# Mixing the modes of eight images in two parts on one Trainium2 core

## The reference

```
# layer 0: a dynamic 3x3 filter per image and group of channels
pooled = x.mean(axis=(2, 3))
lf = tanh(batchnorm(pooled @ conv_w.T))               # 9 taps for each of 8 groups
low = sum over taps of lf * shifted x (reflect padding)
x = (low * (inside + 1) - inside * mean(x)) * lamb_l + x * (lamb_h + 1)
# layer 1: a spectral mix of channels, then a blur
X = dht_2d(x)[:, :, :20, :20]                         # Hartley transform, 20 x 20 modes kept
Y = compl_mul2d(X, w1)                                # for each mode, a 32 x 32 mix of channels
y = dht_2d(Y padded to 128 x 128) / (128 * 128)
y = gaussian blur of y, radius 4, over all four axes  # images, channels, rows, columns
return y * (abs(fftfreq(128)) <= 0.25)                # columns outside the band are zero
```

## Time and profile before

| what | value |
|---|---|
| time, median of 3 runs | 151.3 us (150.71 to 153.71) |
| the profiled execution | 152.74 us |
| its span, first to last instruction | 150.9 us |
| PE busy | 125.7 us (83%), 2308 matmul entries |
| DVE, ACT, POOL busy | 79.8, 40.3, 55.3 us |
| moved by DMA | 37.04 MB |
| mean granted TensorE clock | 0.965 of full speed |

### The profile page before, as it was taken

The page is one execution under the profiler, slowest core; times in us unless marked ns, Lnnn a source line. Parts: engine busy times, 40 slices in busy tenths (PEclk is TensorE's granted clock), DMA queues, the critical chain, the costliest instruction groups (busy, mean ns, idle before and its releaser), DMA issues.

```text
span 150.9 us, 5209 instructions
## 1 busy us (share of the span) xinstructions
PE 125.7 (83%) x2308; PEld 71.9 (48%) x2308; DVE 79.8 (53%) x162; ACT 40.3 (27%) x92; POOL 55.3 (37%) x75
## 2 busy tenths in 40 slices
PE   6496558999999999999899797798797987999500
PEld 5132412655463626257567796465463654654200
DVE  0014840856497969595678114664846748444400
ACT  3000410011112020202599311343242423432300
POOL 8980000399876969699974000000000000000000
PEclk9999997589999999999999999999999999999995
DMA  3999999999999998000000000066998989999994
GB/s 99 358 359 321 295 347 362 348 349 372 371 363 380 351 351 273 11 2 4 0 2 0 4 4 4 4 213 242 312 365 300 384 300 329 350 376 380 386 386 158
DMA packets 34839, 37.04 MB, mean 245 GB/s; under 512 B 1162, under 2 KB 34260, under 8 KB 34816
## 3 DMA queue, kind: packets, MB, share of 16 engines
q1 hardware_dynamic: 34816, 36.70, 72.5%
HBM read 19.92 MB, written 16.78 MB: 243 GB/s over the span
## 4 chain that ended last, share of the span: by engine, by line
PE 28%; POOL 27%; DVE 13%; SPq 9%; DMA 9%; issue 8%; ACT 1%; POOLq 0%; DVEq 0%
PE ps L524 11%; POOL acc L870 5%; DMA x_ring<-x 5%; POOL rows L892 5%; SPq L315 5%; PE ps L464 4%; POOL spread L868 4%; PE ps L485 4%; DVE mixed L789 4%; PE ps L505 4%; DMA out<-rows 4%; DVE xht L726 4%; POOL row_prod L840 3%; POOL eo L878 2%; DVE rows L552 2%
## 5 line engine op out<-in xcount | busy, mean ns | idle before, releaser
L370 PE MATMUL ps<-x_ring,k_lt 64*64 64x512 f32 x256 | 34.7, 646 | 6.9 <-DMA x_ring<-x 6.9
L524 PE MATMUL ps<-cols,k_inv 128*64 128x330 f32 (+1 forms) x192 | 31.5, 466 | 4.5 <-DVE rows L552 4.0
L688 DVE STREAM_TRANSPOSE y_sb<-ps 128x1024 f32<-128x1024 f32 x16 | 19.5, 1241 | 18.2 <-PE ps L370 18.2
L524 PEld LDWEIGHTS ps<-cols,k_inv 128*64 128x64 f32 x192 | 13.3, 136 | 18.3 <-issue 11.8
L552 DVE COPY rows<-ps 128x330 f32<-128x330 f32 (+1 forms) x24 | 12.1, 522 | 12.1 <-PE ps L524 10.6
L388 PEld LDWEIGHTS ps<-y_sb,k_t 64*64 64x64 f32 x512 | 15.5, 143 | 5.0 <-DVE y_sb L688 2.7
L388 PE MATMUL ps<-y_sb,k_t 64*64 64x128 f32 x512 | 17.2, 288 | 0.4 <-ACT kb L589 0.4
L552 ACT COPY rows<-ps 128x330 f32<-128x330 f32 (+1 forms) x24 | 11.0, 462 | 23.7 <-PE ps L524 21.9
L370 PEld LDWEIGHTS ps<-x_ring,k_lt 64*64 64x64 f32 x256 | 8.7, 141 | 16.5 <-issue 9.1
L359 PE MATMUL ps<-idle 128*128 128x256 f32 x52 | 14.6, 431 | 1.2 <-DVE idle L657 1.2
L359 PEld LDWEIGHTS ps<-idle 128*128 128x128 f32 x52 | 10.5, 211 | 3.2 <-DVE idle L657 1.2
(11 more groups left out here) (70 smaller groups left out, 133.4 us busy)
## 6 DMA issues: line engine op xcount, KB each, us to landing
x_ring<-x SPq DMA_DIRECT2D x32, 512.0 KB, 8.7
out<-rows SPq DMA_DIRECT2D x16, 640.0 KB, 5.0
out<-rows SPq DMA_DIRECT2D x8, 768.0 KB, 6.2
w_sb<-mix_w SPq DMA_DIRECT2D x2, 960.0 KB, 10.1
k_inv<-inv SPq DMA_DIRECT2D x1, 386.0 KB, 8.6
k_t<-t SPq DMA_DIRECT2D x1, 256.0 KB, 7.2
k_basis<-basis SPq DMA_DIRECT2D x1, 240.0 KB
k_coef<-coef SPq DMA_DIRECT2D x4, 25.4 KB
```

The costliest lines, as they stand in the source:

```text
L370: last = mm(ps[64 * m:64 * m + 64, 2 * hs + g, :], k_lt[64 * g:64 * g + 64, 64 * r:64 * r + 64], x_ring[64 * g:64 * g + 64, u, k:k + 4, r, ...
L524: last = mm(ps[64 * g:64 * g + 64, B_F[k % 3], 0:nt * NW], inv(O_LH + s * H + r * H // 2, (1, H // 2)), cols[:, u, 6 * g:6 * g + nt, :], s ...
L688: nc.vector.transpose(view(y_sb[:, n % 2, 0, 8 * hs, 0:1], (KINDS, 8), (KINDS * HC, 4), (1, 32)), view(ps[:, 2 * hs, 0:1], (1, 1024))).the ...
```

## The change

The mixing is split. `mixin` keeps 9 columns (8 blurred sums and raw image 5, FIRST = 9), and `mixin_late` takes raw images 6 and 7 (LATE = 2), with `mixed` and `mixed_late` behind them. The first mixing runs in four parts amid the chain that makes the taps and modes of image 7. The late mixing runs in four parts between the first outputs' transforms, as 120 further matmuls of 16 columns. Two of the three `eo` planes move from POOL to DVE. Of the 26 keep_busy matmuls, 14 go. ACT alone copies the parts of both mixings. PSUM banks are dealt anew, the gap memset of DVE moves ahead of the products of image 7, and `shares` takes the raw images from two tiles. The order of the output stage is written out for images 0 and 1, and is the loop above from image 2 on.

```diff
-NCOLS = N + N - BLURRED
+FIRST = N + 1
+LATE = N - BLURRED - 1
@@ the tensor engine's program
             coefficients(N - 2)
             logits(N - 1)
-            keep_busy(4)
-            select(N - 1)
-            keep_busy(2)
-            coefficients(N - 1)
-            keep_busy(8)
-
+            keep_busy(6)
             pe.wait_ge(inv_here, 16)
-            pe.wait_ge(terms_done, N)
-            keep_busy(4)
...
-            pe.wait_ge(placed_act, 4)
-            pe.wait_ge(placed_dve, 3)
+            pe.wait_ge(placed_act, 1)
+            pe.wait_ge(placed_dve, 1)
+            mix(0)
+            select(N - 1)
+            mix(1)
+            coefficients(N - 1)
+            mix(2)
+            mix(3)
...
-            pe.wait_ge(mixed_dve, 2)
-            pe.wait_ge(mixed_act, 2)
+            pe.wait_ge(mixed_act, 4)
             turn(0)
-            keep_busy(2)
+            mix_late(0)
             await_modes(0)
             to_columns(0, 0)
             turn(1)
-            for n in range(N):
+            pe.wait_ge(terms_done, N)
+            pe.wait_ge(row_coef_done, N)
+            to_rows(0, 0, 0, next_columns=True)
+            mix_late(1)
+            to_columns(1, 1)
+            to_rows(0, 0, 1)
+            mix_late(2)
+            mix_late(3)
+            to_rows(1, 1, 0)
+            turn(2)
+            to_rows(1, 1, 1)
+            await_modes(2)
+            to_columns(2, 0)
+            turn(3)
+            for n in range(2, N):
@@ the new late mixing, on the tensor engine
+            def mix_late(part):
+                if part == 0:
+                    pe.wait_ge(late_act, 2)
+                    pe.wait_ge(late_dve, 1)
+                hi, bh = part // 2, part % 2
+                for b in range(5 * bh, 5 * bh + 5):
+                    for q in range(Q):
+                        at = (hi * B10 + b) * 8 * LATE
+                        grp = (hi * Q + q) * B10 + b
+                        for s in range(S):
+                            last = mm(ps[q * C:(q + 1) * C, B_LATE, at:at + 8 * LATE],
+                                      w_sb[:, s * GRP + grp, :], mixin_late[:, grp, 1 - s:3 - s, :, :],
+                                      start=(s == 0), stop=(s == 1))
+                last.then_inc(late_mix_done, 1)
@@ the vector engine's program
+            dve.wait_ge(acc_done, BLURRED)
+            tt(view(eo[:, 0, 1, 0:1], (1, N), (3 * N, GRP)), plus, minus, ALU.add).then_inc(eo_done, 1)
+            tt(view(eo[:, 0, 2, 0:1], (1, N), (3 * N, GRP)), minus, plus, ALU.subtract).then_inc(eo_done, 1)
             total(N - 3)
             turn_columns(N - 1)
+            dve.wait_ge(eo_done, 3)
+            dve.wait_ge(zeroed, 2)
+            place_blurred(nc.vector.tensor_copy, 2)
+            place_blurred(nc.vector.tensor_copy, 3)
+            place(0).then_inc(placed_dve, 1)
             products(N - 2)
             total(N - 2)
@@ the scalar engine's program
+            place(0).then_inc(placed_act, 1)
+            spread_taps(N - 1)
             keep_kb(N - 1)
+            for part in range(4):
+                if part == 2:
+                    keep_row_coef(N - 1)
+                    place(1).then_inc(late_act, 1)
+                act.wait_ge(mix_done, part + 1)
+                unmix(nc.scalar.copy, part // 2, part % 2).then_inc(mixed_act, 1)
+            place(2).then_inc(late_act, 1)
```

More of the change, by code:

```diff
@@ L568, in place_blurred @@
             part = slice(C * cl, C * cl + C)
-            return copy(view(mixin[part, 0, 0, beside(cl), 0:1], (4 * NCOLS, 3 * GRP), (1, N)),
+            return copy(view(mixin[part, 0, 0, beside(cl), 0:1], (4 * FIRST, 3 * GRP), (1, N)),
                         view(eo[part, 0, 0, 0:1], (N, 3 * GRP), (1, N)))
@@ L573, in place_raw @@
             part = slice(C * cl, C * cl + C)
-            return copy(view(mixin[part, 0, 0, beside(cl), N + i:N + i + 1], (4 * NCOLS, 3 * GRP)),
-                        view(eo_raw[part, i, 0, 0:1], (1, 3 * GRP)))
+            if i == 0:
+                to = view(mixin[part, 0, 0, beside(cl), N:N + 1], (4 * FIRST, 3 * GRP))
+            else:
+                to = view(mixin_late[part, 0, 0, beside(cl), i - 1:i], (4 * LATE, 3 * GRP))
+            return copy(to, view(eo_raw[part, i, 0, 0:1], (1, 3 * GRP)))
         @block.scalar
@@ L602, in _ @@
             act.wait_ge(spreads_done, 2)
-            for n in range(1, N + 1):
+            for n in range(1, N):
                 if n >= 2:
@@ L645, in _ @@
             modes_step(1, 1)
-            for n in range(N):
+            rows_step(0, (0, 2))
+            cols_step(1, 1)
+            rows_step(0, (4,))
+            unmix_late_step(0)
+            unmix_late_step(1)
+            rows_step(1, (0, 2))
+            modes_step(2, 0)
+            rows_step(1, (4,))
+            cols_step(2, 0)
+            modes_step(3, 1)
+            for n in range(2, N):
                 rows_step(n, (0, 2))
@@ L739, in place @@
                     last = place_raw(nc.vector.tensor_copy, i, cl)
-                last.then_inc(placed_dve, 1)
+                return last
             turn_rows(0, 0)
@@ L814, in _ @@
             modes_step(1, 1)
-            shares(2)
-            for n in range(N):
+            shares(2, raws[:1])
+            rows_step(0, (1,))
+            cols_step(1, 1)
+            rows_step(0, (3, 5))
+            shares(2, raws[1:])
+            rows_step(1, (1,))
+            modes_step(2, 0)
+            shares(3, raws)
+            rows_step(1, (3, 5))
+            cols_step(2, 0)
+            modes_step(3, 1)
+            shares(4, raws)
+            for n in range(2, N):
                 rows_step(n, (1,))
@@ L870, in blur, with first_plane @@
                 tt(acc[:, lo:hi, :], acc[:, lo:hi, :], spread[:, lo:hi, :], ALU.add).then_inc(acc_done, 1)
[L872 removed]
+            def first_plane():
                 pool.wait_ge(acc_done, BLURRED)
[L874 to L878 removed]
+                tt(view(eo[:, 0, 0, 0:1], (1, N), (3 * N, GRP)), view(acc[:, 0, 0:1], (PLANE, N), (1, GRP)),
+                   view(acc[:, 0, GRP:GRP + 1], (PLANE, N), (1, GRP)), ALU.subtract).then_inc(eo_done, 1)
             def raw_planes(n):
```

133 lines of the change are left out of this document (70 added, 63 removed).

## The result

The changed kernel took **155.38 us**, the median of 4 runs (155.16 to 157.22), against 152.24 us for the kernel before in the same set (4 runs, 150.71 to 153.71). The ratio is 1.0317, 95% interval 1.0179 to 1.0454: slower, clear of noise, though the interval leaves open whether by more than 2%. Single executions of a kernel fall into a faster and a slower group some 2 us apart; a ratio compares the faster ones of both kernels in one set, a median takes all. The prediction had 149.3 us and a range of 145.2 to 152.8. It was wrong, on the wrong side, and outside its range.

What follows compares the result with a forecast made beforehand. Loading of PE's 256-instruction blocks was taken to bound the early outputs: from 77.65 us, 15.0 + 17.6 us reach turn(4) at 110.25 against 112.2. Saving 2 us from the 151.3 us median gave 149.3 us, range 145.2 to 152.8.

Steps and rivals of the forecast that it cites:

- main idea: PE runs in blocks of 256 instructions; waiting for their loading sets the time from the first mixing to turn(4).
- rival without blocks: First rival: blocks don't bind from the mixing to the output loop, so 5.8 us come out, 145.5 us; chance 0.27.
- First mixing 76.6, turn(0) 84.3 us: End of input stage: mixing starts at 76.6 us against 83.97, and turn(0) at 84.3 us, 7.3 us early.
- Hold of POOL by DVE, 1.3 us: Borders of image 5: POOL is held while DVE makes two planes, adding 1.3 us (bounds 0 and 2.5).
- The four quiet blocks, 15.0 us, as the chain: From the boundary at 77.65 us in the first mixing: four blocks of 3.75 us, to 92.65 us.
- The four loaded blocks, 4.4 us each: From 92.65 us to turn(4), beside outputs: four blocks of 4.4 us (between 3.75 and 4.65), 17.6 us, to 110.25.
- The ceiling of 5.1 us: Blocks beside outputs: the most one takes if its packet waits longer, where 4.65 us was the usual loaded price.
- From turn(4) on the loop has its old pace: Output loop behind 110.25 us: unchanged pace, so the 2 us gained by turn(4) come out at the end.
- The clock as a rival of its own: Third rival: TensorE half clock from 84 to 93 us costs 2 to 3 us, 152 us; chance 0.07.
- The second rival: Blocks beside outputs cost 5.1 us each, 152.2 us, or 153.4 with dearer planes; chance 0.14.
- 89.1 + 13.6 us: Without code loading: to_rows(0) at 89.1 us plus 13.6 us of PE work puts to_rows(2) at 102.9 us.

Runs made afterwards that it cites:

- 24: Changed kernel with 6 small one-column matmuls (24 PE instructions) ahead of everything: 153.34 us, ratio 1.0137 to the kernel before.
- 32: Changed kernel with 8 small matmuls (32 PE instructions) ahead of everything: 154.93 us, ratio 1.0204 to the kernel before.
- 48: Changed kernel with 12 one-column matmuls (48 PE instructions) at its very start: 152.53 us, beside 151.89 for the kernel before; no ratio worked out.
- 112: Changed kernel with 28 small matmuls (112 PE instructions) at its start: 151.71 us, ratio 1.0000 to the kernel before.
- planes on POOL: Changed kernel with 48 added instructions, including six keep_busy matmuls at PE's two long waits, and all three planes made on POOL again: 152.89 us, ratio 1.0133.
- shifts 112 and 80 with keepers: Changed kernel with 22 or 14 small matmuls at the start and six keep_busy matmuls at PE's two long waits: 150.47 and 152.18 us, ratios 0.979 and 1.0014.
- late mixing in one piece: Changed kernel with all late mixing ahead of to_columns(0), the loop of before, added keep_busy and 16 small matmuls at the start: 152.51 us, ratio 1.0118.
- the keepers: Three keep_busy matmuls ahead of image 7's logits and three ahead of the late mixing, added to the changed kernel; with 22 small matmuls at the start, ratio 0.979.

## Why the prediction was wrong

Half of its main idea held: PE lives on blocks of 256 instructions, and where a block boundary falls decides much of the time. Its rival without blocks (145.5 us) is refuted. All four shifts of the changed kernel that kept its code as it is (24, 32, 48, 112) moved the stops; the time moved clear of noise at 112. What did not hold is that the blocks are the chain from the first mixing on, and what a block costs beside outputs.

- *First mixing 76.6, turn(0) 84.3 us*: 76.95 and 84.38. Right, but by errors that cancel: the transposition ended 1.7 us earlier in this execution, the planes took 1.4 us each instead of 0.66 (a figure that stood on no row), and six keep_busy took 4.5 instead of 2.7 us at half clock.
- *Hold of POOL by DVE, 1.3 us*: POOL lost 1.6 us beside the planes (0.75 on `row_fn`, 0.8 on `terms`). Right in kind. The Trainium skill (GPSIMD Engine Reference, Specifications) names this contention for operations with two SBUF inputs, and the planes are such: 1.01 us against 0.26 agrees.
- *The four quiet blocks, 15.0 us, as the chain*: PE crosses the boundaries at 77.79, 81.49, 84.72, 88.85 and 92.85 us, 15.06 us in all. The number came out by luck. There is no stop at any of the last four: their packets had ended at 79.36, 82.94, 86.85 and 90.87 us, and 1.35 us more leave PE 0.4 to 0.8 us to spare each time. The steps are 3.7, 3.2, 4.1 and 4.0 us, set by PE's own work, by its waits for ACT (0.73 and 1.37 us) and by the half clock from 86.4 us.
- *The four loaded blocks, 4.4 us each*: 3.8 us to 96.69, where the first short stop stands (0.17 us on PEld), then 5.8 to 102.52, 5.1 to 107.59 and 4.9 to 112.51, together 19.7 instead of 17.6. This is a failed step. The ceiling of 5.1 us "if a packet waits longer" stood on no row and was too low: I had priced a packet that waits for the tail of a transfer, and the one for turn(2) waited for a whole one. The 5.1 us are no price of loading: that packet had ended at 105.53 us, and PE, at half clock, reached the boundary 0.7 us after it could have gone on.
- *"From turn(4) on the loop has its old pace"*: the second failed step, and as large. From that place to the last matmul it is 32.0 us against 29.9. Of the 2.1 us, 1.7 are the two stops of 0.76 and 0.53 with the slower matmuls around them: turn(5) and turn(6) take 1.70 and 1.51 us to the next to_rows instead of 0.76. Their cause is the request behind PE's wait. The rest, some 0.4 us, are three waits for DVE of 0.95 instead of 0.80 us: its additions from two tiles take 0.95 us for two and begin behind one more wait.
- *The clock as a rival of its own (152 us)*: it came on top. Half clock stood from 72.8, 86.4 and 103.5 us, the last right behind the 2.24 us stop, and made to_rows and to_columns there 1.6 us longer, of which 0.7 us count at the next boundary. Half clock follows many of the long stops, but not all: those of 2.25 (planes on POOL), 2.11 and 2.35 us (shifts 112 and 80 with keepers) have full clock behind them.

In sum 2.3 + 2.1 us over the forecast of 150.7 for the profiled execution gives 155.1; 155.16 were measured. The second rival (152.2 to 153.4 us) had the right place and too small a price, and I gave a slowdown of over 2% only 6%. One sum has a slip: 89.1 + 13.6 us puts to_rows(2) at 102.7 us, not 102.9; it moves the first rival by 0.2 us and not the forecast. What I never asked was what another position of the boundaries would do, though I had counted them: fillers alone move this kernel between 1.000 and 1.032 of the kernel before, and with the keepers it reaches 0.979.

The Trainium skill (Runtime: NRT & Kernel Launch, Instruction fetch mechanics) has the next page fetched while the current one executes, mostly hidden. For the wide matmuls of the loop this agrees, with no stop in rows 8. For 128 pairs that take 1.57 us it doesn't, with 2.15 us of stop. In these traces PE stands whenever the work of a block ends less than some 1.3 us behind the end of the next block's packet. That packet is asked for neither on entry nor ahead of a wait within the first 85 instructions.

What stays open: between the 85th and the 93rd instruction the place of the request isn't isolated. Nor is it clear why a packet sometimes goes while a transfer runs and sometimes when it has run out: in the kernel before one goes at 107.87 us, amid data from 103.3 to 108.8 us.

## What to carry to other kernels

Before moving narrow matmuls to an earlier place, count instructions: where PE had to wait for a block here, it came 3.4 to 4.0 us after the entry of the one ahead while no data moved, and up to 5.8 us after it beside the first outputs of the changed kernel, whatever the matmuls' own duration. A change that alters the number of instructions of PE also moves every later boundary; so measure it at two or three alignments, by a few one-column matmuls ahead of everything, before it is called slow or fast. And a long wait shortly behind a boundary is a bad place: 48 instructions ahead of everything took away the stops behind it, though not the one in turn(4).

## What the runs showed that I had not expected

- 28 matmuls that compute nothing take the changed kernel from 1.032 to 1.000 of the kernel before; 53 make the kernel before 1.9% slower.
- PE goes on about 1.3 us behind the end of a packet, which takes 0.9 to 1.2 us in most cases; with the 1.1 to 1.2 us from entry to packet in the late mixing in one piece that is 3.4 to 3.7 us a block.
- The request for a block isn't made on its entry: waits at instruction 53, 73, 77 and 85 are followed by late packets and stops, waits at 93 and beyond aren't.
- An instruction packet can wait for a whole output transfer: 5.8 us from 96.7 to 102.52.
- A one-column matmul with full 128x128 weights cost 0.37 us in a row, mostly at half clock (53 in 19.4 us), a 128x32 one 0.02 us (53 in 1.1 us).
